# Convolution rows by way of DRAM, the spiking neuron worked on in PSUM, and the scan's carries copied by ScalarE

## The chip, the cores and the metric

The kernel runs on one core of a Trainium2 chip. The metric is the device time of one launch in microseconds (us). The kernel before takes 4720.41 us, the median of three runs (4718.8 to 4724.43).

## What is computed

The input is `x`, 8 images of 48 x 48 positions with 256 channels, in float32. Two blocks follow each other, each of them with a group norm in front and its input added to its output.

```python
# block 1: a selective scan
xz = gn(x) @ W_in;  xh, z = split(xz)                 # 512 channels each
xc = depthwise_conv_3x3(xh)                           # SAME padding
dt_r, Bp, Cp = split(xc @ W_xproj)                    # 8, 16, 16
dt = softplus(dt_r @ W_dt + b_dt);  dtN = dt @ W_dtN + b_dtN
h = exp(dt[:, :, None] * A) * h + (dtN * Bp)[:, None, :] * xc[:, :, None]   # per position, 16 states
y = einsum('bdn,bn->bd', h, Cp) + Dskip * xc
x = x + (layernorm(y) * ln_g + ln_b) * silu(z) @ W_out + b_out
# block 2: a leaky integrate-and-fire neuron, its time axis is the batch of 8 images
v = v + (gn(x) @ W.T + b - v) / 2;  s = (v >= 1);  v = v * (1 - s)
out = x + s
```

## The kernel before

An image is cut into 6 row blocks (`K`) of 8 rows, so 384 positions (`T`) each. Channels lie on the 128 partitions, the 512 channels of the scan as 4 groups (`DC`). A row block is worked on in 16 steps, one for each state `n` of the scan (`NS`). In step s of row block k each engine does its share of the main work:

- GpSimd (POOL) multiplies `xc` by a broadcast row of B (`scan_input`, L543), for the state of the next step, and adds the carry of the row block before to the first column (L550). Then it adds the last third of the output to `y` (`accumulate_last`, L590).
- VectorE (DVE) scans 1536 columns as 1024 + 512 (`scan`, L976) and adds two thirds of the output from the transposed states to `y` (`accumulate`, L952). For states 8, 10 and 11 (`OWN`) it adds the last third too (L962).
- TensorE (PE) transposes the scanned states to PSUM (L1097).
- ScalarE (ACT) makes the next decay, exp(dt * A), in PSUM in two parts (`next_decay`, L698), and weighs the last third of the transposed states (`weigh`, L719).

Beside it, the same steps carry the other work, by the table `STEP_GROUPS`: projections, convolution, gate and output matmuls of the neighbouring row blocks. All of it goes through 2 PSUM banks, `work`, which take turns in program order: TensorE fills a bank, another engine empties it, and the next group for that bank waits. Each engine's order is the order of its own loop over k and s; the engines meet by semaphores alone.

The places that the change touches:

- **The convolution.** `xh` of a channel group c is computed by TensorE (steps 0 and 1 for c = 2, 3; steps 13 and 14 for c = 0, 1 of the row block after) and evacuated to `xhp` (L750), 10 rows of 50 columns. SyncE (SP) then copies it to `tri`, where three shifted copies of 32 channels stand on 96 partitions (`copy_rows`, L416): 12 transfers of 50 KB for each c. `tri` has 2 slots, so the copies for c wait until the convolution c - 2 has read its slot. The convolutions (`conv`, L1070) stand in steps 2 to 5.
- **The carry.** GpSimd copies the last column of states 0 to 11 to `carry` (`save_carry`, L567) and multiplies that of states 12 to 15 by the first decay (L569). Both wait for the scan of that state. `decay_carry` (L577) multiplies the 12 kept ones together at step 13. There is no carry over the end of an image, so this runs for row blocks 0 to 4 of each image.
- **The neuron.** For each row block of the image before, TensorE makes two matmul tiles (`l`, one for each 128 output channels) in two steps following each other, at steps 1 and 2 or 9 and 10 of row blocks 1 to 4 (`L1_SLOTS`). VectorE reads each tile and the membrane `volt` (`half_charge`, L913), which empties the bank, then charges (`charge`, L921), adds the spikes to the image (L929) and resets (L932, both in `fire`) over 768 columns in SBUF.
- **Group statistics.** `group_deviation` (L892 to L898) works on 128 x 2 numbers, twice for each image.

## Time and profile before

| | |
|---|---|
| median of 3 runs | 4720.41 us (4718.8 to 4724.43) |
| profiled execution | 4720.14 us, span 4718.4 us |
| TensorE | 3675.9 us (78%) |
| VectorE | 4174.4 us (88%) |
| ScalarE | 3243.7 us (69%) |
| GpSimd | 4161.2 us (88%) |
| mean granted TensorE clock | 0.894 of full speed |

The profile is of one execution. Busy time counts instructions that an engine works on; an instruction's record can overlap the next one's start a little, so the spacing of starts is the better measure of what an instruction costs in a dense stretch. "Idle before" is time in which the engine stood still ahead of an instruction, and the releaser is what ended it. Two engines stand at 88%, and no engine is busy all the time.

### The profile page before, as it was taken

What the parts mean: (1) busy time and instruction counts of PE and PEld (TensorE: products, weight loads), DVE (VectorE), ACT (ScalarE), POOL (GpSimd) and SP (SyncE); (2) the same over time, 40 slices, a digit from 0 to 9 for tenths busy, and PEclk for the clock granted to TensorE, in tenths of its full rate; (3) what the DMA queues carried; (4) which work ended last, traced back from release to release, by engine and by line L of the source; (5) the groups of instructions that cost most, each with busy time, mean ns of one, the idle gap of its engine ahead of it and who ended that gap; (6) DMA issues with size and microseconds to landing.
All of it is one profiled execution on the core that took longest, in us unless ns stands there. A gap on an engine that the chain in (4) does not pass through costs nothing.

```text
span 4718.4 us, 75888 instructions
## 1 busy us (share of the span) xinstructions
PE 3675.9 (78%) x20244; PEld 2302.5 (49%) x20244; DVE 4174.4 (88%) x4013; ACT 3243.7 (69%) x4962; POOL 4161.2 (88%) x3243
## 2 busy tenths in 40 slices
PE   4777777887778878887777878787877888778865
PEld 1444544554445544555544555455544555445543
DVE  0888989999899998998999998999998999999994
ACT  1577777777766777676776777767776767776762
POOL 1899999999898999898999999899999889999991
PEclk8899999898998898888899989898898888999986
DMA  2221221222122222222122222222221222212200
GB/s 58 81 70 59 75 74 52 69 87 76 50 63 79 78 64 63 66 78 78 49 74 70 79 62 70 65 75 64 77 71 61 62 80 73 64 49 83 76 34 20
DMA packets 189431, 315.46 MB, mean 67 GB/s; under 512 B 51993, under 2 KB 164121, under 8 KB 188961
## 3 DMA queue, kind: packets, MB, share of 16 engines
q1 hardware_dynamic: 188960, 310.06, 22.3%
q8 instruction: 189, 3.10, 0.3%
q14 instruction: 282, 2.30, 0.2%
HBM read 171.87 MB, written 20.05 MB: 41 GB/s over the span
## 4 chain that ended last, share of the span: by engine, by line
POOL 31%; issue 26%; PE 19%; DVE 15%; SPq 3%; ACT 3%; DMA 1%; POOLq 1%; DVEq 1%; ACTq 0%
POOL st L543 24%; DVE st L976 10%; PE ht L1097 7%; PE work L1070 3%; SPq L416 3%; DVE y L952 3%; POOL y L590 2%; PE work L1163 2%; POOL carry L567 1%; PE work L1124 1%; POOL xb L599 1%; PE work L1134 1%; PE work L1182 1%; POOL st L550 1%; PE work L1170 1%
## 5 line engine op out<-in xcount | busy, mean ns | idle before, releaser
L976 DVE TENSOR_TENSOR_SCAN st<-decay,st 128x1024 f32<-128x1024 f32 (+1 forms) x1536 | 2727.7, 1776 | 150.1 <-ACT decay L698 66.4
L543 POOL TENSOR_TENSOR st<-xc,bbc 128x1536 f32<-128x1536 f32 x768 | 2662.7, 3467 | 16.3 <-DMA bbc<-brow 11.3
L698 ACT ACTIVATE decay<-dt,neg_a 128x1024 f32<-128x1024 f32 (+1 forms) x1536 | 1357.0, 899 | 459.8 <-DVE st L976 453.5
L1097 PE MATMUL ht<-ident,st 128*128 128x128 f32 x9216 | 1393.4, 305 | 305.9 <-DVE st L976 301.0
L1097 PEld LDWEIGHTS ht<-ident,st 128*128 128x128 f32 x9216 | 1178.8, 157 | 621.8 <-issue 382.8
L952 DVE SCALAR_TENSOR_TENSOR y<-ht,ct,y 128x512 f32<-128x512 f32 x1536 | 1116.2, 727 | 153.5 <-PE ht L1097 151.3
L590 POOL TENSOR_TENSOR y<-y,weighed 128x512 f32<-128x512 f32 x624 | 799.1, 1281 | 185.1 <-ACT weighed L719 181.4
L719 ACT ACTIVATE weighed<-ht,ct 128x512 f32<-128x512 f32 x624 | 426.6, 684 | 364.0 <-PE ht L1097 359.8
L1070 PE MATMUL work<-tri,conv_w 96*32 96x384 f32 x4608 | 485.9, 561 | 151.7 <-issue 87.5
L1129 PE MATMUL work<-xn,win 128*128 128x384 f32 x768 | 315.4, 552 | 112.9 <-DVE ob L913 63.1
L1124 PE MATMUL work<-xn,win 128*128 128x480 f32 x768 | 365.0, 600 | 5.1 <-ACT xn L815 3.1
L1070 PEld LDWEIGHTS work<-tri,conv_w 96*32 96x32 f32 x4608 | 152.4, 120 | 379.1 <-issue 376.5
L1163 PE MATMUL work<-xb,wo 128*128 128x384 f32 x768 | 278.3, 508 | 1.5 <-ACT xb L683 1.5
L1129 PEld LDWEIGHTS work<-xn,win 128*128 128x128 f32 x768 | 154.9, 215 | 225.4 <-DVE ob L913 76.0
L638 POOL TENSOR_TENSOR dt<-xb,dt 128x1536 f32<-128x1536 f32 x48 | 165.2, 3441 | 110.3 <-ACT dt L738 110.3
L599 POOL TENSOR_TENSOR xb<-xb,y 128x384 f32<-128x384 f32 x192 | 200.3, 1065 | 13.7 <-ACT xb L683 13.3
L1124 PEld LDWEIGHTS work<-xn,win 128*128 128x128 f32 x768 | 147.4, 206 | 119.5 <-issue 96.8
L683 ACT ACTIVATE xc<-work 128x384 f32<-128x384 f32 x192 | 92.2, 480 | 160.5 <-PE work L1070 159.9
L1170 PEld LDWEIGHTS work<-skip_diag,xc 128*128 128x128 f32 x1152 | 148.4, 191 | 99.0 <-DVE img L1005 62.5
L550 POOL TENSOR_TENSOR st<-st,cs 128x4 f32<-128x4 f32 x640 | 148.7, 232 | 52.6 <-POOL st L543 4.8
L1163 PEld LDWEIGHTS work<-xb,wo 128*128 128x128 f32 x768 | 148.2, 204 | 85.8 <-issue 13.1
L1146 PE MATMUL work<-xp,wdt 40*128 40x384 f32 x384 | 174.8, 569 | 11.8 <-ACT dt L769 11.0
(96 smaller groups left out, 3692.8 us busy)
## 6 DMA issues: line engine op xcount, KB each, us to landing
bbc<-brow SPq DMA_DIRECT2D x192, 768.0 KB, 4.7
tri<-xhp SPq DMA_DIRECT2D x2304, 50.0 KB, 2.0
...
brow<-xp SPq DMA_DIRECT2D x48, 24.0 KB, 1.5
...
```

The lines of the kernel that those rows point to most:

```text
L543: u = g.tensor_tensor(slot, xc[:, kq % 2, :, :], bbc[:, piece_slot(kq, p), n % PIECE, :].unsqueeze(1).to_broadcast([P, DC, T]), ALU.mult)
L590: g.tensor_tensor(y[:, kq % 2, NTD, :], y[:, kq % 2, NTD, :], weighed[:, n % 2, :], ALU.add).then_inc(s_y2, 1)
L599: g.tensor_tensor(zs[:, c, :], zs[:, c, :], yg[:, c, :], ALU.mult).then_inc(s_yz, 1)
L698: a.activation(flat(decay[:, :, :])[:, lo:hi], flat(dt[:, (k + ahead) % 2, :, :])[:, lo:hi], ACT.Exp, scale=neg_a[:, n:n + 1]).then_inc(s_ ...
L719: a.activation(weighed[:, n % 2, :], ht[:, NTD, :], ACT.Copy, scale=ct[:, kq % 2, NTD * NS + n:NTD * NS + n + 1]).then_inc(s_wt, 1)
L952: v.scalar_tensor_tensor(out=y[:, kq % 2, m, :], in0=ht[:, m, :], scalar=ct[:, kq % 2, m * NS + n:m * NS + n + 1], in1=y[:, kq % 2, m, :], ...
L976: v.tensor_tensor_scan(state[:, lo:hi], flat(decay[:, :, :])[:, lo:hi], state[:, lo:hi], 0.0 if h == 0 else state[:, lo - 1:lo], ALU.mult, ...
L1070: last = t.matmul(work[g * Q:(g + 1) * Q, i, 0:T].rearrange("p (r w) -> p r w", w=W), conv_w[:, c * NQ + g, dx, :], tri[:, c % 2, g, :, dx ...
L1097: last = t.transpose(ht[:, m, c * P:(c + 1) * P], st[:, j, c, m * P:(m + 1) * P], ident[:, :])
L1124: last = t.matmul(work[:, i, 0:HALO], win[:, h, c * P:(c + 1) * P], xn[:, (kc + 1) % 3, h, :], start=h == 0, stop=h == CH - 1)
L1129: last = t.matmul(work[:, i, 0:T], win[:, h, D + c * P:D + (c + 1) * P], xn[:, xn0, h, W:W + T], start=h == 0, stop=h == CH - 1)
L1163: last = t.matmul(work[:, i, 0:T], wo[:, c, h * P:(h + 1) * P], zs[:, c, :], start=c == 0, stop=c == DC - 1)
```

## The change

- **Rows by way of DRAM.** `copy_rows` becomes `put_rows`, one transfer of a channel group's whole `xhp` slot to a DRAM tensor `rows_of_xh` (256 KB), and `get_rows`, three transfers back, one for each row shift, 32 partitions x 4 groups x 400 elements. Each `get_rows` waits for its `put_rows` to land. ScalarE may overwrite an `xhp` slot as soon as the put has landed. In SyncE's order the last B piece of a row block is now loaded between `get_rows` of c = 2 and of c = 3.
- **Carry.** ScalarE copies the last column of all 16 states to `carry`, right behind `next_decay` of the same step. GpSimd only multiplies: states 0 to 11 at step 13, states 12 to 15 at step 2 of the row block after. `scan_input` waits for ScalarE's copy of the state three before.
- **Neuron.** The membrane is kept doubled for each image so that the halving falls away (`units` holds the scale; the weights and the bias are scaled by it). `charge_and_fire` adds in the PSUM tile itself and then writes the spikes, each for 384 columns; it stands between the second half of the scan and `accumulate` of the second third. ScalarE copies the tile to `volt` (`copy_membrane`), and `reset` on VectorE, at the place where `half_charge` stood, reads the tile once more and only then empties the bank.
- **Statistics.** `group_deviation` keeps its intermediate values in the PSUM bank, with one more instruction, and gives the bank back at its end.

```diff
...
@@ -404,17 +409,24 @@
                              ot[:, :, :]).then_inc(s_out, 16)
-            def copy_rows(b, k, c):
-
+            def put_rows(b, k, c):
+
+                qc = b * K + k + 1
                 await_emptied(sp, b, k, f"xh{c}")
+                need(sp, s_tri[c], qc * STEPS * 16)
                 hold("sp", sp, b)
-
+                sp.dma_start(rows_v[c], xhp[:, c % 3, :, :].rearrange("p r w -> p (r w)")).then_inc(s_put[c], 16)
+
+            def get_rows(b, k, c):
+
+                qc = b * K + k + 1
                 await_filled(sp, b, k if c > 1 else k - 1, f"cv{(c - 2) % DC}")
+                sp.wait_ge(s_put[c], (qc + 1) * 16)
                 hold("sp", sp, b)
-                for g in range(NQ):
-                    for dy in range(TAPS):
-                        sp.dma_start(tri[dy * Q:(dy + 1) * Q, c % 2, g, :, :],
-                                     xhp[g * Q:(g + 1) * Q, c % 3, dy:dy + ROWS, :]).then_inc(s_tri[c], 16)
+                for dy in range(TAPS):
+                    sp.dma_start(tri[dy * Q:(dy + 1) * Q, c % 2, :, :, :].rearrange("i g r w -> i g (r w)"),
+                                 rows_v[c].rearrange("(g i) e -> i g e", i=Q)[:, :, dy * WP:(dy + ROWS) * WP]
+                                 ).then_inc(s_tri[c], 16)
...
@@ -462,8 +477,10 @@
                 if PRE2 in do:
-                    copy_rows(*following(b, k), 0)
-                    copy_rows(*following(b, k), 1)
+                    put_rows(*following(b, k), 0)
+                    put_rows(*following(b, k), 1)
+                    get_rows(*following(b, k), 0)
+                    get_rows(*following(b, k), 1)
...
@@ -546,35 +565,21 @@
                     pool.wait_ge(s_ux, (bq * (K - 1) + kq - 1) * NS + n + 1)
-                    pool.wait_ge(s_cs, (bq * (K - 1) + kq - 1) * NCS + 1 + max(0, n - NCOPY + 1))
+                    pool.wait_ge(s_cs, (bq * (K - 1) + kq - 1) * 2 + (1 if n < NCOPY else 2))
                     g.tensor_tensor(st[:, j, :, 0], st[:, j, :, 0], cs[:, :, n], ALU.add).then_inc(s_u, 1)
                 else:
                     u.then_inc(s_u, 1)
-            def saved(e, n):
-
-                if n < NCOPY:
-                    pool.wait_ge(s_carry, e * NCOPY + n + 1)
-                else:
-                    pool.wait_ge(s_cs, e * NCS + 1 + n - NCOPY + 1)
-
-            def save_carry(b, k, n):
-
-                last = st[:, (k * NS + n) % 3, :, T - 1]
-                pool.wait_ge(s_scan, (b * K + k) * NS + n + 1)
-                if n < NCOPY:
-                    hold("pool", pool, b)
-                    g.tensor_copy(carry[:, :, n], last).then_inc(s_carry, 1)
-                else:
-                    g.tensor_tensor(cs[:, :, n], last, a0[:, :, n], ALU.mult).then_inc(s_cs, 1)
-
-            def decay_carry(b, k):
-
-                e = b * (K - 1) + k
+            def decay_carry(b, k, e, lo, hi):
+
                 pool.wait_ge(s_a0, e + 1)
-                pool.wait_ge(s_u, (b * K + k) * NS + NCOPY)
-                pool.wait_ge(s_carry, (e + 1) * NCOPY)
-                g.tensor_tensor(cs[:, :, 0:NCOPY], carry[:, :, 0:NCOPY], a0[:, :, 0:NCOPY], ALU.mult).then_inc(s_cs, 1)
+                pool.wait_ge(s_carry, e * NS + hi)
+                if lo == 0:
+                    pool.wait_ge(s_u, (b * K + k) * NS + NCOPY)
+                elif k > 1:
+                    pool.wait_ge(s_u, (b * K + k) * NS)
+                hold("pool", pool, b)
+                g.tensor_tensor(cs[:, :, lo:hi], carry[:, :, lo:hi], a0[:, :, lo:hi], ALU.mult).then_inc(s_cs, 1)
...
@@ -706,6 +712,14 @@
                     a.activation(dt[:, p1, :, 0], far[:, :], ACT.Copy).then_inc(s_far, 1)
+                def save_carry(n):
+
+                    e = b * (K - 1) + k
+                    act.wait_ge(s_scan, (b * K + k) * NS + n + 1)
+                    need(act, s_cs, (e - 1) * 2 + (1 if n < NCOPY else 2))
+                    hold("act", act, b)
+                    a.activation(carry[:, :, n], st[:, (k * NS + n) % 3, :, T - 1], ACT.Copy).then_inc(s_carry, 1)
+
...
@@ -802,6 +816,13 @@
                         bank_copy(name, dst, n * C, view=lambda v, n=n: v.rearrange("p (m c) -> p m c", m=n))
+
+                def copy_membrane(kc, h):
+
+                    act.wait_ge(s_spike, ((b - 1) * K + kc) * CH + h + 1)
+                    hold("act", act, b)
+                    i = turn(b, k, f"l{kc}_{h}")[0]
+                    a.activation(volt[:, h, kc * T:(kc + 1) * T], work[:, i, 0:T], ACT.Copy).then_inc(s_kept, 1)
@@ -858,6 +879,11 @@
                     next_decay(s)
+                    if main and k < K - 1:
+                        save_carry(s)
+                    for kc, a0_step in (L1_SLOTS.get(k, ()) if L1 in do else ()):
+                        if s in (a0_step, a0_step + 1):
+                            copy_membrane(kc, s - a0_step)
@@ -889,20 +915,24 @@
                 i = await_filled(dve, b, k, f"gm{w}")
-                v.tensor_copy(gn_mu[w][:, :], work[:, i, 0:CH]).then_inc(emptied[i], 1)
-                await_emptied(dve, b, k, f"gm{w}")
-                v.tensor_tensor(gn_dm[w][:, :], gn_mv[w][:, :, 0], gn_mu[w][:, :], ALU.subtract).then_inc(s_gdv[w], 1)
-                dve.wait_ge(s_gdv[w], e * 3 + 1)
-                v.tensor_tensor(gn_sq[w][:, :], gn_dm[w][:, :], gn_dm[w][:, :], ALU.mult).then_inc(s_gdv[w], 1)
-                dve.wait_ge(s_gdv[w], e * 3 + 2)
-                v.tensor_tensor(gn_dv[w][:, :], gn_sq[w][:, :], gn_mv[w][:, :, 1], ALU.add).then_inc(s_gdv[w], 1)
+                mean, off, square = (work[:, i, j * CH:(j + 1) * CH] for j in range(3))
+                v.tensor_copy(gn_mu[w][:, :], mean)
+                v.tensor_tensor(gn_dm[w][:, :], gn_mv[w][:, :, 0], mean, ALU.subtract).then_inc(s_gdv[w], 1)
+                v.tensor_tensor(off, gn_mv[w][:, :, 0], mean, ALU.subtract).then_inc(s_gdv[w], 1)
+                dve.wait_ge(s_gdv[w], e * 4 + 2)
+                v.tensor_tensor(square, off, gn_dm[w][:, :], ALU.mult).then_inc(s_gdv[w], 1)
+                dve.wait_ge(s_gdv[w], e * 4 + 3)
+                v.tensor_tensor(gn_dv[w][:, :], square, gn_mv[w][:, :, 1], ALU.add).then_inc(s_gdv[w], 1)
+                dve.wait_ge(s_gdv[w], e * 4 + 4)
+                dve.sem_inc(emptied[i], 1)
             def group_variance(w, b, k):
                 i = await_filled(dve, b, k, f"gv{w}")
                 v.tensor_scalar(gn_ve[w][:, :], work[:, i, 0:CH], GN_EPS, None, ALU.add).then_inc(emptied[i], 1)
-            def half_charge(b, k, kc, h):
-
+            def charge_and_fire(b, k, kc, h):
+
+                il = ((b - 1) * K + kc) * CH + h
@@ -910,27 +940,24 @@
                 i = await_filled(dve, b, k, f"l{kc}_{h}")
-                v.scalar_tensor_tensor(out=ob[:, h, :], in0=work[:, i, 0:T], scalar=b1s[:, h:h + 1],
-                                       in1=volt[:, h, cols], op0=ALU.add, op1=ALU.subtract).then_inc(emptied[i], 1)
-
-            def charge(b, k, kc):
+                now = work[:, i, 0:T]
+                v.scalar_tensor_tensor(out=now, in0=now, scalar=b1s[:, h:h + 1], in1=volt[:, h, cols],
+                                       op0=ALU.add, op1=ALU.add).then_inc(s_volt, 1)
+                dve.wait_ge(s_volt, il + 1)
+                hold("dve", dve, b)
+                v.scalar_tensor_tensor(out=ob[:, h, :], in0=now, scalar=units[:, 1:2],
+                                       in1=img[:, img_par(b, -1), h, cols], op0=ALU.is_ge,
+                                       op1=ALU.add).then_inc(s_spike, 1)
+
+            def reset(b, k, kc, h):
                 cols = slice(kc * T, (kc + 1) * T)
-                for h in range(CH):
-                    await_emptied(dve, b, k, f"l{kc}_{h}")
-                v.scalar_tensor_tensor(out=volt[:, :, cols], in0=ob[:, :, :], scalar=0.5,
-                                       in1=volt[:, :, cols], op0=ALU.mult, op1=ALU.add).then_inc(s_volt, 1)
-
-            def fire(b, k, kc):
-
-                il = (b - 1) * K + kc
-                cols = slice(kc * T, (kc + 1) * T)
-                dve.wait_ge(s_volt, il * 2 + 1)
-                v.scalar_tensor_tensor(out=ob[:, :, :], in0=volt[:, :, cols], scalar=1.0,
-                                       in1=img[:, img_par(b, -1), :, cols], op0=ALU.is_ge,
-                                       op1=ALU.add).then_inc(s_spike, 1)
-                v.scalar_tensor_tensor(out=volt[:, :, cols], in0=volt[:, :, cols], scalar=1.0,
-                                       in1=volt[:, :, cols], op0=ALU.is_lt, op1=ALU.mult).then_inc(s_volt, 1)
+                dve.wait_ge(s_kept, ((b - 1) * K + kc) * CH + h + 1)
+                hold("dve", dve, b)
+                i = turn(b, k, f"l{kc}_{h}")[0]
+                now = work[:, i, 0:T]
+                v.scalar_tensor_tensor(out=volt[:, h, cols], in0=now, scalar=units[:, 1:2], in1=volt[:, h, cols],
+                                       op0=ALU.is_lt, op1=ALU.mult).then_inc(emptied[i], 1)
@@ -987,6 +1014,10 @@
                             scan(b, k, s, h)
+                        if h == 1 and L1 in do:
+                            for kc, a in L1_SLOTS.get(k, ()):
+                                if s in (a, a + 1):
+                                    charge_and_fire(b, k, kc, s - a)
@@ -1014,11 +1045,7 @@
                             if s in (a, a + 1):
-                                half_charge(b, k, kc, s - a)
-                            if s == a + 1:
-                                charge(b, k, kc)
-                            if s == a + 2:
-                                fire(b, k, kc)
+                                reset(b, k, kc, s - a)
...
```

SyncE in row block 0 of the middle images, from the loop's first transfer (L416 are the copies to `tri`, L437 loads a piece of B, L426 writes B rows; the ISA and REGISTER_ALU rows are waits). Before:

```order
L314 REGISTER_ALU
L416 DMA tri<-xhp 32x400 x12
L321 ISA
L314 REGISTER_ALU
L416 DMA tri<-xhp 32x400 x12
L302 ISA
L437 DMA bbc<-brow 128x1536
```

And now (L418 is the put, L427 the gets, L449 the piece of B):

```order
L307 ISA
L418 DMA rows_of_xh<-xhp 128x500
L326 ISA
L418 DMA rows_of_xh<-xhp 128x500
L319 REGISTER_ALU
L424 ISA
L427 DMA tri<-rows_of_xh 32x4x400 x3
L307 ISA
L449 DMA bbc<-brow 128x1536
L319 REGISTER_ALU
L427 DMA tri<-rows_of_xh 32x4x400 x3
```

24 transfers in a row have become two puts and twice three gets, and the wait for the convolution's slot (L314, now L319) has moved behind both puts.

VectorE in step 9 of row block 2, with the first neuron tile of that slot (L976 is the scan, L952 and L962 add to `y`). Before:

```order
L976 SCALAR_TENSOR_TENSOR st<-decay,st 128x512
L940 REGISTER_ALU
L947 REGISTER_ALU
L952 SCALAR_TENSOR_TENSOR y<-ht,ct,y 128x512
L960 REGISTER_ALU
L962 SCALAR_TENSOR_TENSOR y<-ht,ct,y 128x512
L314 REGISTER_ALU x2
L913 SCALAR_TENSOR_TENSOR ob<-work,b1s,volt 128x384
```

And now (the scan is L1003, the additions to `y` are L979 and L989):

```order
L1003 SCALAR_TENSOR_TENSOR st<-decay,st 128x512
L319 REGISTER_ALU x2
L944 SCALAR_TENSOR_TENSOR work<-work,b1s,volt 128x384
L946 ISA
L948 ISA
L948 SCALAR_TENSOR_TENSOR ob<-work,units,img 128x384
L967 REGISTER_ALU
L974 REGISTER_ALU
L979 SCALAR_TENSOR_TENSOR y<-ht,ct,y 128x512
L987 REGISTER_ALU
L989 SCALAR_TENSOR_TENSOR y<-ht,ct,y 128x512
L959 SCALAR_TENSOR_TENSOR volt<-work,units,volt 128x384
```

Two instructions have come in ahead of the additions to `y`, and one stands where the single one stood; the three wide ones of the steps after (L921, L929, L932) are gone.

GpSimd in two steps of row block 1 of a middle image. Before:

```order
L564 REGISTER_ALU
L567 COPY carry<-st 128x4
L302 REGISTER_ALU
L557 REGISTER_ALU
L543 TENSOR_TENSOR st<-xc,bbc 128x1536
L548 REGISTER_ALU
L550 TENSOR_TENSOR st<-st,cs 128x4
L589 REGISTER_ALU
L590 TENSOR_TENSOR y<-y,weighed 128x512
```

Of these rows L564 (the wait for the scan) and L567 are no longer there in the changed order; the others stand as before.

## Rows read from the trace of the kernel before

**Rows 1.** The page, part 1: span, then busy time and instructions of each engine.

```profile
span 4718.4 us, 75888 instructions
PE 3675.9 (78%) x20244; PEld 2302.5 (49%) x20244; DVE 4174.4 (88%) x4013; ACT 3243.7 (69%) x4962; POOL 4161.2 (88%) x3243
```

**Rows 2.** Windows of one image: columns are length, busy per engine, clock, DMA.

```profile
1248.26:1336.99 88.73, 69.80 (x401) 42.93 (x400) 80.22 (x77) 65.14 (x101) 82.58 (x59) 0.92 0.22 65
...
1435.19:1536.55 101.36, 81.18 (x446) 51.78 (x444) 91.06 (x90) 69.31 (x109) 89.22 (x72) 0.90 0.24 70
...
sum 568.38, PE 452.25 PEld 284.90 DVE 522.34 ACT 404.63 POOL 520.64; mean PE 75.38 PEld 47.48 DVE 87.06 ACT 67.44 POOL 86.77
```

**Rows 3.** Timeline, DVE, two scans one step apart.

```profile
1717.79 2.27 DVE L976 TENSOR_TENSOR_SCAN st<-decay,st 128x1024 f32<-128x1024 f32 x1
...
1722.48 2.29 DVE L976 TENSOR_TENSOR_SCAN st<-decay,st 128x1024 f32<-128x1024 f32 x1
```

**Rows 4.** Timeline, POOL, one carry copy and what follows it.

```profile
1656.83 0.20 POOL L567 COPY carry<-st 128x4 f32<-128x4 f32 x1
1656.97 3.46 POOL L543 TENSOR_TENSOR st<-xc,bbc 128x1536 f32<-128x1536 f32 x1
```

**Rows 5.** Timeline, SP, PE, DVE and POOL, around 1637 to 1662 us.

```profile
1637.11 16.56 SPq L416 DMA_DIRECT2D tri<-xhp  x24
...
1655.10 2.14 PE L1070 MATMUL work<-tri,conv_w 96*32 96x384 f32 x24 [1.43 <-issue]
...
1660.06 0.75 DVE L952 SCALAR_TENSOR_TENSOR y<-ht,ct,y 128x512 f32<-128x512 f32 x1 [1.92 <-PE ht L1097]
...
1661.60 1.27 POOL L590 TENSOR_TENSOR y<-y,weighed 128x512 f32<-128x512 f32 x1 [0.89 <-ACT weighed L719]
```

**Rows 6.** The page, part 6: DMA issues, KB each, us to landing.

```profile
tri<-xhp SPq DMA_DIRECT2D x2304, 50.0 KB, 2.0
brow<-xp SPq DMA_DIRECT2D x48, 24.0 KB, 1.5
```

**Rows 7.** Groups by form: busy us, mean ns, idle before and its releasers.

```profile
L1070 PE MATMUL work<-tri,conv_w 96*32 96x384 f32 x4608 | 485.9, 561 | 151.7 <-issue 87.5 <-DMA tri<-xhp 60.7 <-ACT xc L683 2.0
L952 DVE SCALAR_TENSOR_TENSOR y<-ht,ct,y 128x512 f32<-128x512 f32 x1536 | 1116.2, 727 | 153.5 <-PE ht L1097 151.3
```

**Rows 8.** Timeline, PE, start of the span, 78 to 100 us.

```profile
78.47 4.07 PE L1070 MATMUL work<-tri,conv_w 96*32 96x384 f32 x24 [5.12 <-DMA tri<-xhp]
...
95.05 4.07 PE L1070 MATMUL work<-tri,conv_w 96*32 96x384 f32 x24 [4.00 <-DMA tri<-xhp]
```

**Rows 9.** Groups by form, as Rows 7: small copies and carries.

```profile
L567 POOL COPY carry<-st 128x4 f32<-128x4 f32 x480 | 119.5, 249 | 41.9 <-DVE st L976 39.6
...
L707 ACT ACTIVATE dt<-far 128x4 f32<-128x4 f32 x48 | 9.5, 199 | 0.0
```

**Rows 10.** Groups by form, DVE: the neuron and the group statistics.

```profile
L932 DVE SCALAR_TENSOR_TENSOR volt<-volt 128x768 f32<-128x768 f32 x48 | 59.1, 1232 | 0.0
L929 DVE SCALAR_TENSOR_TENSOR ob<-volt,img 128x768 f32<-128x768 f32 x48 | 59.0, 1229 | 0.2
L913 DVE SCALAR_TENSOR_TENSOR ob<-work,b1s,volt 128x384 f32<-128x384 f32 x96 | 58.5, 610 | 37.4 <-PE work L1182 37.4
L921 DVE SCALAR_TENSOR_TENSOR volt<-ob,volt 128x768 f32<-128x768 f32 x48 | 54.8, 1142 | 5.4
...
L894 DVE TENSOR_TENSOR gn_dm<-gn_mv,gn_mu 128x2 f32<-128x2 f32 x16 | 28.9, 1803 | 0.6
...
L898 DVE TENSOR_TENSOR gn_dv<-gn_sq,gn_mv 128x2 f32<-128x2 f32 x16 | 18.1, 1133 | 0.6
```

**Rows 11.** L894 by source: count, ns min/median/max, first and last start us.

```profile
L894 DVE TENSOR_TENSOR gn_dm<-gn_mv,gn_mu x16: 160/916/3292, 53.3 to 4650.3; 128x2 f32<-128x2 f32 x16
```

**Rows 12.** Timeline, DVE scan of step 9 and the ACT decay behind it.

```profile
1678.25 1.27 DVE L976 TENSOR_TENSOR_SCAN st<-decay,st 128x512 f32<-128x512 f32 x1
...
1680.83 1.71 ACT L698 ACTIVATE decay<-dt,neg_a 128x1024 f32<-128x1024 f32 x2
```

49 lines of the change are left out of this document (31 added, 18 removed).

## The prediction

> **What bounds the kernel now.** I read the page first [rows 1]: VectorE and GpSimd each work 88% of the span, ScalarE 69%. Two engines at the same share, with 12% idle on both, mean that neither bounds alone; they wait for each other and for TensorE. Then the windows of one image [rows 2]: the six row blocks take 568.4 us, 94.7 each, with VectorE busy 87.1, GpSimd 86.8 and ScalarE 67.4. A row block without neuron work takes 88.7 us, one with two neuron slots 101.4. Over one step, a dense stretch of VectorE takes 1722.48 - 1717.79 = 4.69 us [rows 3]; GpSimd has about the same, and a carry copy in it shifts the next instruction by 1656.97 - 1656.83 = 0.14 us, call it 0.15 [rows 4].
>
> Then I followed the largest idle on VectorE back by timelines. In the middle of a row block [rows 5], SyncE issues 24 copies to `tri` in one go, 16.56 us, 0.69 each. The 12 for c = 3 are the last, so they end at 1653.67 and the last convolution starts at 1655.10, after 1.43 us of idle on TensorE (the row says issue; what it waits for is the transfer's landing, 2.0 us after its issue [rows 6]). The transposes behind it come late, VectorE stands for 1.92 us at 1660.06, and GpSimd for 0.89 us at 1661.60. All the idle of this kind is 151.7 us ahead of the convolutions on TensorE and 151.3 us on VectorE for transposes [rows 7].
>
> **The change, part by part.**
>
> *Rows by way of DRAM.* The wait for the free `tri` slot stays where it was, but behind it stand now 3 issues instead of 12: 3 x 0.69 and the landing, where 12 x 0.69 + 2.0 = 10.3 us were needed. The put is outside of this, since it needs only the evacuated `xhp`, several us earlier. The trace has one comparable transfer to DRAM, 24 KB in 1.5 us, and one of 50 KB in 2.0 [rows 6]; 256 KB and 200 KB will take more, I take 3 us each, so 2.1 + 3 = 5.1 us from the free slot to the landing. The c = 2 rows then land at about 1637.1 + 5.1 = 1642, and those of c = 3, whose slot is freed one convolution later, at about 1646: 9 us ahead of 1655.1, and still ahead if the B piece in front of them takes twice as long as they do. So the wait ahead of the convolutions ends. At the start, where nothing covers it, the three waits are 5.12 (first) to 4.00 us (last), 13.6 together [rows 8]; less than a us of each should stay: -12 us (bounds -13.6 and 0). Of the 138 us that are left in the 48 row blocks, part is passed on. VectorE's waits for transposes have other causes too (banks held by the neuron and by the dt evacuations), so I take -95, two thirds of what TensorE loses; bounds 0 and -140.
>
> The page "DMA: Bandwidth & Descriptors", section "Anatomy of one DMA — SWDGE (gpsimd) path", of the Trainium skill says that about 2 us of a transfer are fixed, nearly all of it the receipt of the write, and that DRAM is the heaviest target. It speaks against sending rows there and back. The 1.5 us of the write to DRAM here is not heavier than the 2.0 on chip, and by either figure the put has landed before the slot is free.
>
> *Carry.* GpSimd loses 480 copies (12 states in 40 row blocks) and 160 products (4 states), 640 instructions at 0.15 us of spacing = 96 us, and gains 40 products, 6 us: 90 us of its time, beside 39.6 us in which the copies waited for the scan [rows 4, 9]. GpSimd and VectorE are equally loaded [rows 2], so what one gains counts until the other is in front: I take half, -45; bounds 0 and -130. ScalarE gets 640 copies of 128x4; such a copy is 0.20 us [rows 9], 128 us in all, 2.7 for each row block. It is hidden by the 27 us that ScalarE is idle in one [rows 2], and stands behind the decay of its step, so that the next scan does not wait for it. Behind the copy are the late evacuations and the next `weigh`, for which TensorE and GpSimd wait; 0.2 us there is inside the noise of their order. Without that cover it would cost up to its 128 us. GpSimd's new wait is for a copy made two steps before.
>
> *Neuron.* Before, VectorE spends 58.5 + 54.8 + 59.1 + 59.0 = 231 us on 48 charges [rows 10]. Now there are 6 instructions of 384 columns for each, every one with a PSUM operand like L913's 610 ns: 288 x 0.61 = 176 us, and 96 waits between charge and spikes of some 0.15: 190 us, so -41. What L921, L929 and L932, all with two SBUF inputs, lose to delays is in their means and so in the 41.
>
> The Trainium skill has a rule for each side. "SBUF — State Buffer", section "Who interferes with whom", says that a VectorE instruction with two SBUF inputs and a GpSimd instruction that reads SBUF exclude each other; by that rule the delays of L894 and of the wide instructions go away altogether. The trace agrees for L894: the same two columns take 0.16 us or up to 3.29 [rows 11]. "VectorE: DVE Perf Modes", in the section on the TRN2 errata, gives a PSUM operand a higher fixed cost for each instruction (120 cycles against 58), which speaks against two half-width instructions in place of a wide one. The rows have that price in them: two of L913 are 1.22 us, one L929 1.23.
>
> Against the 41 stand new waits. `reset` waits for ScalarE's copy of the tile, which is behind the decay. In step 9 ScalarE is late: the scan ends at 1679.52, and both decays end at 1682.54 [rows 12]. The copy, a quarter of a decay's columns and so about 0.5 us with its start, ends at about 1683.1, while VectorE, after 1.4 us for charge and spikes and 1.3 for two additions, is ready at 1682.2: some 1.2 us of stall with the semaphores, in the 24 slots that begin at step 9, 29 us. The tile itself is now needed before the additions to `y`, 0.65 to 1.3 us sooner, and it came late in 16 cases of 96 [rows 10]: 6 us. Sum of the neuron: -6; bounds -55 (no new wait) and +75 (1.2 us in all 96). Behind the held bank stands the z projection of step 10; it comes 1.2 us later and just makes its reader.
>
> *Statistics.* L894 and L898 take 47.0 us for 32 instructions on two columns, which undisturbed take 0.16 [rows 10, 11]: some 42 us go, 2.6 come for the added one. The bank is held about 0.9 us longer, and GpSimd's input is then often the next thing missing: -22, bounds -45 and 0.
>
> Sum: -12 - 95 - 45 - 6 - 22 = -180 us, from the profiled execution's 4720.14: 4540. That execution is 0.3 us from the median of the runs, so nothing is added for the difference.
>
> **The rivals.**
>
> A, nearly all of it reaches the path, because VectorE and GpSimd wait for each other and gain together: 4720 - 13.6 - 130 - 80 - 6 - 38 = 4452, say 4455. For it speaks that both are idle at the same place in [rows 5]; against it that no chain gives back all its waits. Chance 12%.
>
> B, the rows come no sooner, since put and get are in series and share the queue with the pieces of B: both first terms fall away, 4720 - 45 - 6 - 22 = 4647. Against it stand 5.1 us in the place of 10.3. Chance 10%.
>
> C, the neuron's waits on ScalarE cost 1.2 us in both kinds of slot, 115 us against the 41 saved, +74, with the other terms as they are: 4720 - 174 + 74 = 4620. Chance 10%.
>
> D, ScalarE becomes the pace. Its queue is in order, and the 640 copies and the 96 of 0.5 us (48 us) are all in front of some `weigh` on which TensorE's and GpSimd's next work hangs. In full this is +128 + 48 = +176, and it swallows the gains of rows and carry since these are then behind ScalarE; where a third of it lands, 4720 + 59 - 12 = 4767, slower than before. It decides once ScalarE's idle in a row block is under the waits that it can't fill, and 27 - 3.7 = 23 us are far from that. Chance 5%.
>
> **How the numbers follow.** Forecast 63%, A 12%, B 10%, C 10%, D 5%. The predicted time is 4540 us, that of the likeliest; its own range is 4490 to 4595. From A up to B the range is 4455 to 4650, which leaves out D and the outer tails, somewhat under 2 in 10. A change of 0.2% is 9 us, about the least that a measurement of this kernel can tell. All cases but D lie far over it: faster 93%, same 2%, slower 5%.
>
> **What would show it.** Right: the idle ahead of the convolutions down from 151.7 to under 30 us; VectorE's wait for transposes from 151 to some 60; L921, L929, L932 gone and VectorE's busy time near 4095; GpSimd's near 4020; ScalarE's at 3420; the row blocks without neuron work at about 84.5 us and those with two slots 2.5 to 4 less than now. A wait of `reset` for ScalarE's copy should be there, some 30 us in all. Wrong would be: a convolution that still waits for `tri` (B), more than 80 us of idle ahead of `reset` or of the charge (C), VectorE's waits for the decay grown by more than all others shrink (D).

## The result, and the profile after

| | before | after |
|---|---|---|
| median | 4722.42 us (4 runs) | 4574.31 us (4568.55 to 4578.71, 4 runs) |
| ratio to before, same chip | | 0.9689, 95% interval 0.9675 to 0.9703 |
| profiled execution | 4720.14 us | 4570.02 us |
| granted TensorE clock, mean | 0.894 | 0.916 |

The kernel is 3.1% faster, some 148 us; the forecast was 4540 us, 180 less than before. The granted clock rose too, and the runs of one kernel are shorter at a higher clock (the kernel after: 4568.55 us at 0.917, 4578.71 at 0.909). At that rate, 10 us for 0.008, the 0.022 between before and after would be some 28 us; this is an estimate, and no run separates what came with the clock from what raised it. The page of the kernel after, part 1, answers to [rows 1]:

```profile
span 4568.0 us, 74518 instructions
PE 3595.8 (79%) x20244; PEld 2243.1 (49%) x20244; DVE 4081.0 (89%) x4077; ACT 3338.8 (73%) x5698; POOL 4007.6 (88%) x2661
```

VectorE works 93 us less, and stands idle 57 us less (span less busy: 544 before, 487 now). Windows of the kernel after, the same image as in [rows 2], its row blocks 0, 2 and 3 (columns: length, busy for each engine, clock, DMA):

```profile
1194.36:1276.96 82.60, 66.61 (x401) 40.00 (x400) 79.08 (x76) 66.46 (x116) 80.31 (x43) 0.98 0.27 82
...
1368.10:1464.63 96.53, 78.25 (x443) 48.92 (x441) 88.67 (x90) 72.47 (x128) 83.48 (x57) 0.93 0.29 86
1464.63:1562.83 98.20, 76.61 (x438) 49.38 (x438) 89.58 (x92) 72.78 (x129) 83.63 (x58) 0.91 0.29 85
...
sum 549.90, PE 442.99 PEld 277.95 DVE 509.79 ACT 416.80 POOL 499.71; mean PE 73.83 PEld 46.33 DVE 84.97 ACT 69.47 POOL 83.28
```

The sum fell from 568.4 to 549.9. Over the whole run, from one row block's layernorm sum on GpSimd to the next, the mean periods over all images went, by row block 0 to 5, from 88.6, 97.1, 96.5, 96.7, 93.7, 87.7 to 82.9, 90.9, 95.5, 96.1, 92.6, 85.2 us. Row blocks 0 and 1 gained 6 each, 2 to 5 only 1.1, 0.6, 1.1 and 2.5. On average it is 93.49 to 90.70, 131 us over 47 periods; the start gives 23 more (the first of these sums came at 228.94 us and comes at 205.93), and the tail takes 4 back.

The groups by form of the kernel after answer to [rows 7, 9, 10] (columns: busy us, mean ns, idle before and its releasers):

```profile
L1099 PE MATMUL work<-tri,conv_w 96*32 96x384 f32 x4608 | 430.0, 507 | 19.0 <-ACT xc L689 13.1 <-DMA tri<-rows_of_xh 4.3 <-ACT y L793 1.6
L1158 PE MATMUL work<-xn,win 128*128 128x384 f32 x768 | 340.9, 588 | 133.2 <-DVE volt L959 100.7 <-DVEq L927 16.5 <-ACT xb L689 13.6
...
L1003 DVE TENSOR_TENSOR_SCAN st<-decay,st 128x1024 f32<-128x1024 f32 x768 | 1752.8, 2282 | 167.5 <-ACT decay L704 75.1 <-POOL st L569 43.8 <-POOL st L562 30.9
L979 DVE SCALAR_TENSOR_TENSOR y<-ht,ct,y 128x512 f32<-128x512 f32 x1536 | 1121.6, 730 | 94.7 <-PE ht L1126 94.4
L948 DVE SCALAR_TENSOR_TENSOR ob<-work,units,img 128x384 f32<-128x384 f32 x96 | 59.3, 618 | 19.8 <-DVE work L944 19.0
L959 DVE SCALAR_TENSOR_TENSOR volt<-work,units,volt 128x384 f32<-128x384 f32 x96 | 59.2, 617 | 26.1 <-ACT volt L825 20.6
L944 DVE SCALAR_TENSOR_TENSOR work<-work,b1s,volt 128x384 f32<-128x384 f32 x96 | 58.4, 608 | 34.3 <-PE work L1211 34.2
L925 DVE TENSOR_TENSOR gn_dv<-work,gn_mv 128x2 f32<-128x2 f32 x16 | 2.5, 159 | 0.5
L920 DVE TENSOR_TENSOR gn_dm<-gn_mv,work 128x2 f32<-128x2 f32 x16 | 2.4, 151 | 0.0
```

The convolutions wait 19.0 us in all, where it was 151.7. The statistics' two instructions take 0.15 us each. VectorE's wait for transposes fell only to 94.4. TensorE's z matmuls (L1158) now stand 100.7 us for the neuron's reset (L959). The same matmuls waited before, for the instruction that emptied the neuron's bank then (L913), but 63.1 us:

```profile
L1129 PE MATMUL work<-xn,win 128*128 128x384 f32 x768 | 315.4, 552 | 112.9 <-DVE ob L913 63.1 <-DVE gn_ve L902 19.8 <-DVE gn_mu L892 17.1
```

The page's part 6 answers to [rows 6] (KB each, us to landing):

```profile
bbc<-brow SPq DMA_DIRECT2D x192, 768.0 KB, 6.1
tri<-rows_of_xh SPq DMA_DIRECT2D x576, 200.0 KB, 3.9
rows_of_xh<-xhp SPq DMA_DIRECT2D x192, 250.0 KB, 2.6
```

SyncE's timeline of the kernel after, in the row block that answers to [rows 5] (start us, us, queue, line):

```profile
1565.06 0.32 SPq L418 DMA_DIRECT2D rows_of_xh<-xhp  x1
1569.19 1.27 SPq L427 DMA_DIRECT2D tri<-rows_of_xh  x3
1570.67 0.34 SPq L449 DMA_DIRECT2D bbc<-brow  x1
1576.23 1.25 SPq L427 DMA_DIRECT2D tri<-rows_of_xh  x3
```

Three transfers from DRAM are issued in 1.25 us, 0.42 each, where one on chip took 0.69 in [rows 5]. Over the whole run the median record of one such issue is 0.59 us before (2304 of them) and 0.43 after (576).

### The profile page after: what moved, and what is told of

The parts are those of the page before. It is cut to its first block, busy times and chain, and to the rows that moved or that the text cites. A ratio compares the mean times of both kernels' runs of the same rounds, so it can differ in the third digit from the quotient of the medians.

```text
span 4568.0 us, 74518 instructions
## 1 busy us (share of the span) xinstructions
PE 3595.8 (79%) x20244; PEld 2243.1 (49%) x20244; DVE 4081.0 (89%) x4077; ACT 3338.8 (73%) x5698; POOL 4007.6 (88%) x2661
## 4 chain that ended last, share of the span: by engine, by line
POOL 33%; issue 26%; PE 16%; DVE 16%; ACT 7%; DVEq 1%; POOLq 1%; DMA 1%; SPq 0%; ACTq 0%
POOL st L562 27%; DVE st L1003 11%; PE ht L1126 6%; DVE y L979 2%; PE work L1192 2%; POOL y L595 2%; PE work L1158 2%; ACT decay L704 2%; PE work L1163 1%; PE work L1153 1%; POOL xb L604 1%; POOL st L569 1%; PE work L1199 1%; DVE work L944 1%; PE work L1099 1%
## 5 line engine op out<-in xcount | busy, mean ns | idle before, releaser
L1003 DVE TENSOR_TENSOR_SCAN st<-decay,st 128x1024 f32<-128x1024 f32 (+1 forms) x1536 | 2732.4, 1779 | 167.6 <-ACT decay L704 75.1
L1126 PE MATMUL ht<-ident,st 128*128 128x128 f32 x9216 | 1372.4, 300 | 448.4 <-DVE st L1003 370.7
L1126 PEld LDWEIGHTS ht<-ident,st 128*128 128x128 f32 x9216 | 1145.5, 154 | 775.5 <-issue 439.7
L979 DVE SCALAR_TENSOR_TENSOR y<-ht,ct,y 128x512 f32<-128x512 f32 x1536 | 1121.6, 730 | 94.7 <-PE ht L1126 94.4
L1158 PE MATMUL work<-xn,win 128*128 128x384 f32 x768 | 340.9, 588 | 133.2 <-DVE volt L959 100.7
L1099 PE MATMUL work<-tri,conv_w 96*32 96x384 f32 x4608 | 430.0, 507 | 19.0 <-ACT xc L689 13.1
L1158 PEld LDWEIGHTS work<-xn,win 128*128 128x128 f32 x768 | 168.0, 234 | 257.9 <-DVE volt L959 115.3
L1099 PEld LDWEIGHTS work<-tri,conv_w 96*32 96x32 f32 x4608 | 135.4, 112 | 221.7 <-issue 213.5
L604 POOL TENSOR_TENSOR xb<-xb,y 128x384 f32<-128x384 f32 x192 | 188.8, 1000 | 31.8 <-ACT xb L689 31.7
L1199 PE MATMUL work<-skip_diag,xc 128*128 128x128 f32 x1152 | 155.2, 278 | 38.6 <-DVE img L1036 38.5
L1211 PE MATMUL work<-img,w1s 128*128 (+1 forms) x384 | 170.1, 574 | 14.9 <-DVE volt L959 7.8
L569 POOL TENSOR_TENSOR st<-st,cs 128x4 f32<-128x4 f32 x640 | 133.2, 208 | 55.2 <-POOL st L562 9.7
```

The source lines that it names most:

```text
L979: v.scalar_tensor_tensor(out=y[:, kq % 2, m, :], in0=ht[:, m, :], scalar=ct[:, kq % 2, m * NS + n:m * NS + n + 1], in1=y[:, kq % 2, m, :], ...
L1003: v.tensor_tensor_scan(state[:, lo:hi], flat(decay[:, :, :])[:, lo:hi], state[:, lo:hi], 0.0 if h == 0 else state[:, lo - 1:lo], ALU.mult, ...
L1099: last = t.matmul(work[g * Q:(g + 1) * Q, i, 0:T].rearrange("p (r w) -> p r w", w=W), conv_w[:, c * NQ + g, dx, :], tri[:, c % 2, g, :, dx ...
L1126: last = t.transpose(ht[:, m, c * P:(c + 1) * P], st[:, j, c, m * P:(m + 1) * P], ident[:, :])
L1158: last = t.matmul(work[:, i, 0:T], win[:, h, D + c * P:D + (c + 1) * P], xn[:, xn0, h, W:W + T], start=h == 0, stop=h == CH - 1)
L1199: last = t.matmul(work[:, i, c * P:(c + 1) * P], xc[:, par, c, m * P:(m + 1) * P], skip_diag[:, c, :], start=True, stop=True)
```

## The experiments

All times are medians of 5 to 12 runs (4 for the whole change), all ratios are to the kernel before on the same chip. "us" is what the ratio makes of 4722.5 us, less 4722.5. VectorE's busy time and the reset's mean are from one profiled execution of each kernel; that of all but neuron took 4681.1 us, 23 more than the median of its kernel.

| kernel | median | ratio, 95% interval | us | VectorE busy | reset, mean ns |
|---|---|---|---|---|---|
| rows alone | 4620.1 | 0.9784 (0.9757 to 0.9812) | -102 | 4172 | 1233 |
| carry alone | 4779.5 | 1.0116 (1.0090 to 1.0143) | +55 | 4232 | 2835 |
| neuron alone | 4741.7 | 1.0037 (1.0019 to 1.0055) | +17 | 4129 | 617 |
| statistics alone | 4679.9 | 0.9907 (0.9881 to 0.9932) | -44 | 4134 | 1216 |
| carry and neuron | 4747.7 | 1.0049 (1.0031 to 1.0067) | +23 | 4115 | 617 |
| all but carry | 4594.2 | 0.9713 (0.9694 to 0.9732) | -136 | 4086 | 617 |
| all but neuron | 4658.4 | 0.9860 (0.9839 to 0.9880) | -66 | 4209 | 2979 |
| rows and statistics | 4585.3 | 0.9705 (0.9684 to 0.9726) | -139 | 4133 | 1231 |
| the whole change | 4574.3 | 0.9689 (0.9675 to 0.9703) | -147 | 4081 | 617 |

The old reset is one instruction over 768 columns, the new one two over 384.

**One part alone, four times.** Each kernel is the one before with a single part of the change as the diff above has it.

> The kernel before with the rows by way of DRAM alone; carry, neuron and statistics as before. The changed kernel starts its first row block 23 us earlier (228.9 to 205.9 us), and its idle ahead of the convolutions is 19 us where it was 152. Theory 1 (rows are the largest part): the start is 20 us or more earlier and each row block some 1.5 to 2 us shorter, so 4720 - 20 - 85 = about 4615, with the idle ahead of the convolutions under 40 us. Rival 2 (GpSimd sets the pace, so that the wait ahead of the convolutions was hidden): only the start is won, 4695 to 4700, and GpSimd's waits for the weighed tile fall while its busy time per row block stays.

> The kernel before with the carries copied by ScalarE alone. Theory 1: half of GpSimd's 90 us reaches the path, about 4675, since the late convolution of each row block still makes all engines wait. Rival 2 (GpSimd sets the pace): nearly all of the 90 us and part of the 40 us of waits for the scan, 4620 or less. Rival 3 (the copies on ScalarE delay its evacuations): no gain, 4715 or more, with longer waits of VectorE for the decay than the 66 us of before.

> The kernel before with the neuron in PSUM alone. Theory 1: VectorE loses about 50 us of work, but the bank that is held until the reset delays the z projection of step 10, the transposes behind it and VectorE's step 11, by 1.4 to 1.8 us in each of the 24 row blocks with a slot at step 9; net between -15 and +25 us, 4705 to 4745. Rival 2 (the neuron's work is on the path and the held bank is covered): -40 us or more, 4680 or less, and no wait of VectorE for transposes in step 11.

> The kernel before with the group statistics in PSUM alone. Theory 1: 35 to 40 us less VectorE work in 16 places, half of it on the path: about 4700. Rival 2 (nothing of it on the path): 4715 to 4725. Whether the four singles add up to the whole (148 us) tells whether the parts overlap: below 148 together they help each other, above they save the same waits.

The characteristic line of each:

```diff
 # rows alone
-STEPS = NQ * 3
+STEPS = TAPS
 # carry alone
+                    if main and k < K - 1:
+                        save_carry(s)
 # neuron alone
-                                half_charge(b, k, kc, s - a)
+                                reset(b, k, kc, s - a)
 # statistics alone
-                v.tensor_tensor(gn_dm[w][:, :], gn_mv[w][:, :, 0], gn_mu[w][:, :], ALU.subtract).then_inc(s_gdv[w], 1)
+                v.tensor_tensor(gn_dm[w][:, :], gn_mv[w][:, :, 0], mean, ALU.subtract).then_inc(s_gdv[w], 1)
```

Rows alone bring 102 us, 19 of them at the start, and at a clock of 0.892 to 0.895, so not by the clock. Statistics bring 44, twice what was expected (about 4700 us): all that VectorE was held for. Neuron alone costs 17 though VectorE is busy 45 us less: its wait for transposes grows from 151 to 202 us, and new waits ahead of the spikes and the reset come to 39.5 (17.7 and 21.8). Carry alone costs 55, where a gain was forecast: taking work off GpSimd made the kernel slower. The single parts add up to -74; the whole is -147, so two or more of them help each other.

The group by form of the kernel with the carry alone shows where its loss begins (columns as above; before it was 59.1 us, mean 1232):

```profile
L925 DVE SCALAR_TENSOR_TENSOR volt<-volt 128x768 f32<-128x768 f32 x48 | 136.1, 2835 | 0.0
```

**Carry and neuron; all but carry.** The same parts, combined.

> The kernel before with the carry and the neuron changed, rows and statistics as before. Alone they cost 54 us and 16 to 18 us. Theory 1 (the carry alone was slower because GpSimd, no longer held by its wait for the scan, then collides with VectorE's wide instructions with two SBUF inputs: the reset of the neuron took 2835 ns on average instead of 1232): with the neuron in PSUM there is nothing left to collide with but the statistics, so the carry gains 30 to 50 us over the neuron alone (4742), and this runs at 4690 to 4715. Rival 2 (the copies on ScalarE are what costs, by delaying its evacuations and weighed tiles): the costs add, 4790 or more.

> The changed kernel with the carries left on GpSimd. Theory 1: without collisions the carry is worth 30 to 50 us, so 4605 to 4625. Rival 2: the carry costs here too, 4530 or less. Rival 3 (neither): within 10 us of 4574.

```diff
 # all but carry: the copies stay on GpSimd
+            def save_carry(b, k, n):
+                last = st[:, (k * NS + n) % 3, :, T - 1]
...
+                    g.tensor_copy(carry[:, :, n], last).then_inc(s_carry, 1)
```

With the neuron's new form the carry costs next to nothing more (+23 beside +17; the intervals touch), and the reset stays at 617 ns. It gains nothing either without the rows: VectorE waits 235.5 us for transposes. So both forecasts of this kernel missed, the gain of 30 to 50 us once the collisions are gone as well as the sum of the losses: the collisions explain why the carry alone costs 55, and taking them away does not make the lighter GpSimd pay. In the whole, the carry is worth 20 us by the medians and 11 by the ratios, whose intervals overlap a little, where 30 to 50 were expected.

**All but neuron; rows and statistics.** These complete the four combinations of carry and neuron on top of the other two parts.

> The changed kernel with the neuron as before the change (rows, carry and statistics changed). Theory 1, the neuron's new form is what takes the collision out of reset and of the wide membrane instructions once GpSimd has no carry copies: the wide L9xx instructions collide again, VectorE's busy time goes up by 80 to 150 us to about 4180, and the time is 4605 to 4630 us, 30 to 55 slower than the changed kernel. Theory 2, the rows' faster arrival has already given the engines another phase and the collision is gone with it: then the neuron costs in the whole what it costs alone (16 us), and the time is 4550 to 4565, faster than the changed kernel.

> Only rows and statistics changed, carry and neuron as before the change. Sum of the two measured alone: 4722 - 106 - 46 = 4570 us, within 5 us of the whole change, and with that the neuron and the carry together are worth nothing. Rival, taken from the two runs that stand beside it: the kernel without the carry's part is at 4594, and if the neuron there gives what it gives with the others (30 to 50), this one is at 4625 to 4645. Told apart by the time, and by the mean of the wide L9xx instructions on VectorE (1232 ns before).

```diff
 # all but neuron
-                                reset(b, k, kc, s - a)
+                                half_charge(b, k, kc, s - a)
+                            if s == a + 1:
+                                charge(b, k, kc)
+                            if s == a + 2:
+                                fire(b, k, kc)
```

On top of rows and statistics (4585) the carry alone costs 73 us (4658), the neuron alone 9 (4594, intervals overlapping), and both together gain 11 (4574; 8 by the ratios, intervals overlapping). Read the other way: rows and statistics by themselves have 139 of the 147 us, and what carry and neuron add together is not clear of the noise. Rows and statistics came out between the two times expected (4570, and 4625 or more). All but neuron has the direction of the first theory, but not its size (4605 to 4630). The reset's mean is near 3 us in the one corner with ScalarE's carry and the old neuron, as without rows and statistics; in all the others it is undisturbed or at its old mean. Timelines of VectorE and GpSimd of the kernel without the neuron's part show one such case:

```profile
1604.37 1.21 DVE L939 SCALAR_TENSOR_TENSOR ob<-volt,img 128x768 f32<-128x768 f32 x1
1605.50 4.20 DVE L942 SCALAR_TENSOR_TENSOR volt<-volt 128x768 f32<-128x768 f32 x1
```

```profile
1604.72 4.17 POOL L556 TENSOR_TENSOR st<-xc,bbc 128x1536 f32<-128x1536 f32 x1
```

L942 over SBUF alone takes 0.95 us at its least. Here it ends at 1609.70, 0.81 after GpSimd's multiply (1608.89): it ran once that had ended. The multiply too took 4.17 instead of 3.45, since L939 was at work until 1605.58. The same place in the kernel before, VectorE and then GpSimd:

```profile
2640.18 1.22 DVE L929 SCALAR_TENSOR_TENSOR ob<-volt,img 128x768 f32<-128x768 f32 x1
2641.32 0.94 DVE L932 SCALAR_TENSOR_TENSOR volt<-volt 128x768 f32<-128x768 f32 x1
```

```profile
2640.52 0.92 POOL L567 COPY carry<-st 128x4 f32<-128x4 f32 x1
2641.41 4.16 POOL L543 TENSOR_TENSOR st<-xc,bbc 128x1536 f32<-128x1536 f32 x1
```

There the small carry copy is what stands on GpSimd while the spikes (L929) are written; the reset gets its turn behind the copy, and the multiply is the one that waits for the reset. Without the copy the multiply itself stands there, and the reset waits for all of it. The timelines of all 48 resets of a kernel bear this out: GpSimd is in the multiply when the reset starts in none of them before the change and in none with rows and statistics, in 23 with the carry alone and in 26 without the neuron's part, and each of these 49 resets ends 0.81 to 0.82 us after the multiply.

**Bank freed early.** Charge writes `volt` at once, spikes and reset read SBUF, and ScalarE's 96 copies fall away.

> The changed kernel, but charge_and_fire adds the tile and the membrane straight into volt, which frees the bank at once; spikes and reset then read volt (384 columns, two SBUF inputs each), and ScalarE's 96 membrane copies fall away. Theory 1, what the neuron's part costs is the bank held until reset: the wait of z's matmuls for volt (100 us) goes to under 10, VectorE's wait at step 11 ends, and the time is 4535 to 4555 us. Rival, the two instructions with two SBUF inputs wait for GpSimd again as the lone carry change showed it (2.8 us where 1.2 are needed): reset's mean is over 1000 ns for 384 columns, VectorE's busy time rises by over 60 us and the time is 4590 or more.

```diff
-                v.scalar_tensor_tensor(out=now, in0=now, scalar=b1s[:, h:h + 1], in1=volt[:, h, cols],
-                                       op0=ALU.add, op1=ALU.add).then_inc(s_volt, 1)
+                v.scalar_tensor_tensor(out=volt[:, h, cols], in0=now, scalar=b1s[:, h:h + 1], in1=volt[:, h, cols],
+                                       op0=ALU.add, op1=ALU.add).then_inc(emptied[i], 1)
...
-                v.scalar_tensor_tensor(out=ob[:, h, :], in0=now, scalar=units[:, 1:2],
+                v.scalar_tensor_tensor(out=ob[:, h, :], in0=volt[:, h, cols], scalar=units[:, 1:2],
...
-                v.scalar_tensor_tensor(out=volt[:, h, cols], in0=now, scalar=units[:, 1:2], in1=volt[:, h, cols],
-                                       op0=ALU.is_lt, op1=ALU.mult).then_inc(emptied[i], 1)
+                v.scalar_tensor_tensor(out=volt[:, h, cols], in0=volt[:, h, cols], scalar=units[:, 1:2],
+                                       in1=volt[:, h, cols], op0=ALU.is_lt, op1=ALU.mult).then_inc(s_kept, 1)
```

It took 4722.83 us, ratio 1.0001 (0.9990 to 1.0012): 148 us slower than the changed kernel, as much as the whole gain. The rival is right. Its groups by form:

```profile
L945 DVE SCALAR_TENSOR_TENSOR ob<-volt,units,img 128x384 f32<-128x384 f32 x96 | 198.1, 2063 | 17.8 <-DVE volt L941 16.9
L952 DVE SCALAR_TENSOR_TENSOR volt<-volt,units 128x384 f32<-128x384 f32 x96 | 132.2, 1377 | 0.0
```

The same columns take 618 and 617 ns with the tile in PSUM. VectorE is busy 205 us more (4285.6). VectorE's stop at step 11 did go, so the held bank was its cause, but z's matmuls still wait 76.1 us, now for the charge. With the carry on ScalarE, reading the tile in PSUM is what the neuron's part is worth: not fewer columns, but an operand for which VectorE doesn't have to wait. This kernel is even 64 us slower than the one with the old neuron (4658), and its VectorE is busy 77 us more: it has twice as many spike and reset instructions with two SBUF inputs.

**Second half of the slot moved; slot moved by one.** The held bank shows in the kernel after. Timelines of TensorE and VectorE, steps 10 and 11 of row block 3:

```profile
1516.87 1.45 PE L1158 MATMUL work<-xn,win 128*128 128x384 f32 x4
1524.11 2.92 PE L1158 MATMUL work<-xn,win 128*128 128x384 f32 x4 [5.79 <-DVE volt L959]
```

```profile
1523.44 0.62 DVE L959 SCALAR_TENSOR_TENSOR volt<-work,units,volt 128x384 f32<-128x384 f32 x1
1523.98 2.28 DVE L1003 TENSOR_TENSOR_SCAN st<-decay,st 128x1024 f32<-128x1024 f32 x1
1527.79 0.75 DVE L979 SCALAR_TENSOR_TENSOR y<-ht,ct,y 128x512 f32<-128x512 f32 x1 [1.53 <-PE ht L1126]
```

TensorE's z matmuls stand 5.79 us for the second tile's reset, the transposes of step 11 queue behind them, and VectorE stands 1.4 to 1.8 us in row blocks 1 to 3.

> The changed kernel with the second half of the neuron's slot at step 9 moved from step 10 to step 12, so that the z projections of step 10 no longer take over a bank that the reset gives back late. Theory 1 (the held bank costs VectorE its wait for transposes of 1.4 to 1.8 us in step 11 of 24 row blocks, and TensorE 5.9 us): that wait is gone and 20 to 40 us with it, 4535 to 4555, unless the outputs of step 13, which now wait for the reset of step 12, give a part back. Rival 2 (VectorE would be waiting for GpSimd at this place in any case): within 5 us of 4574, with the idle moved to the scan's wait for its input.

> The changed kernel with the neuron's slots of steps 9 and 10 moved to 8 and 9; steps 10 and 11, where the z matmuls and the late transposes stand, then find both banks free. Theory 1, the 1.4 to 1.8 us that VectorE stands for transposes at step 11 come from the second tile's bank held into step 10: they go, in 24 slots, and the time is 4540 to 4560. Rival, the place of the slot only moves the wait (in step 8 VectorE has the last third to add as well): 4570 to 4600, with the same idle at step 9 or 10.

```diff
 # second half at step 12
+HALVES = {1: (1, 2), 9: (9, 12)}
...
-        if s in (a, a + 1):
-            dve.append((L1, f"l{kc}_{s - a}"))
+        if s in HALVES[a]:
+            dve.append((L1, f"l{kc}_{HALVES[a].index(s)}"))
 # slot at steps 8 and 9
-L1_SLOTS = {1: ((0, 9),), 2: ((1, 1), (2, 9)), 3: ((3, 1), (4, 9)), 4: ((5, 1),)}
+L1_SLOTS = {1: ((0, 8),), 2: ((1, 1), (2, 8)), 3: ((3, 1), (4, 8)), 4: ((5, 1),)}
```

Neither brought the gain that its first theory forecast; the rival of the second (4570 to 4600, the wait only moves) holds. The first took 4625.39 us (ratio 0.9786, 0.9767 to 0.9805), 51 more than the changed kernel; the second 4599.37 (0.9740, 0.9721 to 0.9760), 25 more. In both the stop at step 11 is gone. In the first, VectorE stands 2.3 to 2.6 us for the tile at step 12 and 1.2 to 2.8 us for an output matmul at step 13. In the second, the charge waits for its tile, 86.4 us in all where it was 34.3:

```profile
L944 DVE SCALAR_TENSOR_TENSOR work<-work,b1s,volt 128x384 f32<-128x384 f32 x96 | 58.8, 613 | 86.4 <-PE work L1211 86.3
```

With two banks a wait of this kind moves to the next user; neither of the two places tried is better than the present one.

**Twelve transfers from DRAM.** The changed kernel with its three gets cut into twelve.

> The changed kernel with each block's rows read back from DRAM in 12 transfers of 50 KB instead of 3 of 200 KB. Theory 1 (what delayed the convolutions was SyncE's issuing, 0.69 us for each of 12 transfers in a row): most of what the rows won is lost, 60 to 90 us, 4635 to 4665, with the idle ahead of the convolutions back at 100 us or more. Rival 2 (it was the transfer on chip itself, 2.0 us to land, or that it had to wait for its slot): 4575 to 4590.

```diff
-                for dy in range(TAPS):
...
+                for g in range(NQ):
+                    for dy in range(TAPS):
...
+                                     rows_v[c][g * Q:(g + 1) * Q, dy * WP:(dy + ROWS) * WP]
```

It took 4597.9 us (ratio 0.9738, 0.9719 to 0.9756), 24 more than with three. That is between the two times expected (4635 or more, and up to 4590), and the count explains only that much of the 102 us that the rows bring alone. The first layernorm sum comes at 223.39 us, 17.5 later than with three; the periods of the row blocks differ by 0.24 us each, some 11 in all. The timeline of SyncE and the group of the convolutions say why:

```profile
1571.39 12.79 SPq L428 DMA_DIRECT2D tri<-rows_of_xh  x24
...
1591.45 5.42 SPq L428 DMA_DIRECT2D tri<-rows_of_xh  x12
```

```profile
L1100 PE MATMUL work<-tri,conv_w 96*32 96x384 f32 x4608 | 447.0, 523 | 64.7 <-DMA tri<-rows_of_xh 38.2 <-issue 18.3 <-ACT xc L690 7.7
```

They are issued at 0.45 us each (twelve in 5.42) to 0.53 (24 in 12.79), not 0.69 [rows 5] as on chip. The idle ahead of the convolutions rises by 46 us; 13 of them fall before the first layernorm sum, and of the 33 in the row blocks these hide two thirds. My expectation had charged the twelve at the on-chip issue. What the rest of the rows' gain comes from was not separated: the cheaper issue of each transfer, or that an `xhp` slot is free once one put has landed.

## Why the prediction came out as it did

The time was inside the range, and within the forecast's own range. It was 34 us too fast. The rows, the largest part, came out as worked out; that the total is so near is in part luck, since the statistics brought more than forecast and carry and neuron together less.

- **Start, forecast -12.** With rows alone the first layernorm sum comes 19.4 us earlier, with the whole change 23.0; the first scan starts at 118.61 us, 14.1 earlier. The three waits of 4 to 5 us [rows 8] became 0.42, 0.42 and 3.28 us, so one of them kept more than the us allowed for:

```profile
71.89 2.14 PE L1099 MATMUL work<-tri,conv_w 96*32 96x384 f32 x24 [0.42 <-DMA tri<-rows_of_xh]
...
79.88 3.84 PE L1099 MATMUL work<-tri,conv_w 96*32 96x384 f32 x24 [3.28 <-DMA tri<-rows_of_xh]
84.31 2.14 PE L1099 MATMUL work<-tri,conv_w 96*32 96x384 f32 x24 [0.60 <-ACT xc L689]
```

  The waits were not the whole price. Each convolution behind one of them ran at a granted clock of 0.50 (1.2 GHz) and took 4.07 us; now three of the four take 2.14 at 1.00 (2.4 GHz), and only the one behind the wait of 3.28 us takes 3.84, at 0.55. That is another 4 us. With the rows alone the waits were short too, 2.0, 1.1 and 0.6 us, but the last three convolutions still took 4.07 each, so the clock doesn't follow from the last wait alone. The second row block too had waits for rows, 4.8 us, which are 0.2 now.
- **Rows in the row blocks, -95.** Alone they brought 102 less 19 = 83. The chain [rows 5] was read rightly: the idle ahead of the convolutions is 19.0, under the 30 given. The landings were 2.6 (put) and 3.9 us (get) where 3 each was taken; the issues were cheaper, 0.42. B falls.
- **Carry, -45.** Wrong in its mechanism, the step that failed: "what one gains counts until the other is in front". It is worth 11 to 20 us in the whole (intervals overlapping), nothing beside the neuron alone, and +55 and +73 with the old neuron. GpSimd's time did fall as forecast, to 4007.6 (4020 given). What I left out is that GpSimd's copies decide which of its instructions the reset meets, and that [rows 10, 11] already had the price of a bad phase in them: L894, 0.16 to 3.29 us. I used those rows only for the instructions that go away, not to ask which remaining one might meet it more often.
- **Neuron, -6.** Alone it is +17, and in the whole -84 by the medians (4658.42 to 4574.31). Its saving was in the 41, from old means; but with ScalarE's carry the reset's 1232 ns would have become 2979, and it is the neuron's part that prevents that. This only cancels the carry's failure: the two forecast together -51, and brought -8 to -11 on top of rows and statistics. The split in two halves has a price that the old mean hid: a wide instruction that meets nothing takes 0.95 us, two half-width ones 1.22. It is not the PSUM operand: with the bank freed early, the half-width reset with both inputs in SBUF took 0.60 us at its least and 0.61 in the median, against 0.62 in PSUM. The higher fixed cost for a PSUM operand that the Trainium skill gives ("VectorE: DVE Perf Modes", the section on the TRN2 errata) doesn't show here. What makes two halves dearer than one wide instruction was not separated (the halves also take their scalar from a tile). Of the waits, reset's for ScalarE was 20.6 us (30 given). The step "comes 1.2 us later and just makes its reader" is wrong: z's matmuls wait up to 6.1 us, and VectorE 1.4 to 1.8 us behind them. Row blocks with two slots gained 1.1 and 0.6 us, not 2.5 to 4; the 101.4 us of [rows 2] is one image's, and the mean of that row block before was 96.5. C is not what happened, since the waits ahead of charge and reset are 54.8 us, under its 80, but its kind of loss is real, one engine further on.
- **Statistics, -22.** Alone -44, twice the forecast and at its lower bound of -45; on top of the rows -37 (0.9784 to 0.9705). VectorE was held 41 us less (4174.4 to 4133.6), and none of it was given back; halving it had no row behind it.
- **ScalarE.** Busy 3338.8, not 3420. D is far: VectorE's wait for the decay went from 66.4 to 75.1 us. A timeline of ScalarE after shows that the copy can cost half of what its record says:

```profile
1508.35 0.20 ACT L721 ACTIVATE carry<-st 128x4 f32<-128x4 f32 x1
1508.45 0.56 ACT L782 ACTIVATE xb<-work,bdt 128x384 f32<-128x384 f32 x1
```

The next instruction starts 0.10 us after it. For GpSimd I had taken the spacing, for ScalarE the duration.

Row blocks without neuron work are at 84.1 us on average (82.9 and 85.2), where 84.5 was given; VectorE at 4081 (4095).

Open: how much of VectorE's 94.4 us for transposes could be had by a third bank was not tried, the rows' worth in the whole change (all but rows) was not run, and the clock's share of the gain was not separated.
